# Splitting W2's products around the row scores, and one transpose for both tiles' row maxima

## What is computed

```python
x = x + _L0_xattn_ref(_layernorm(x), ctx, ...)   # 16 heads, 64 keys; then relu(out @ W1 + b1) @ W2 + b2
x = x + _L0_ffn_ref(_layernorm(x), ...)          # top 2 of 8 LoRA experts around one 256->1024->256 FFN
x = x + _L1_xattn_ref(_layernorm(x), ctx, ctx, ...)
x = x + _L1_ffn_ref(x, weight, disha)
```

```python
q = (x @ Wq + bq).reshape(B, N, NUM_HEADS, HEAD_DIM)
scores = jnp.einsum('bnhd,bmhd->bhnm', q, k) * scale
attn = jax.nn.softmax(scores, axis=-1)
out = jnp.einsum('bhnm,bmhd->bnhd', attn, v).reshape(B, N, IMAGE_DIM)
h = jax.nn.relu(out @ W1 + b1)
return h @ W2 + b2
```

## Time and profile before

| | |
|---|---|
| median of 3 runs | 336.73 us (336.33 to 340.38) |
| the profiled execution's own time | 335.96 us |
| its span in the trace | 333.9 us |
| TensorE busy (products) | 316.3 us, 95% |
| VectorE, ScalarE, GpSimd busy | 233.0, 172.2, 145.1 us |
| share of the last chain on TensorE | 86% |
| mean granted TensorE clock | 0.987 of full |

### The profile page before, as it was taken

How to read it: one execution, slowest core, us unless ns; L and a number is a source line. 1 busy time by engine, 2 the same in 40 slices (tenths; PEclk the granted TensorE clock), 3 DMA queues, 4 the chain that set the end, 5 groups by cost and what they waited for, 6 DMA issues and landing times.

```text
span 333.9 us, 6495 instructions
## 1 busy us (share of the span) xinstructions
PE 316.3 (95%) x2515; PEld 287.9 (86%) x2515; DVE 233.0 (70%) x643; ACT 172.2 (52%) x347; POOL 145.1 (43%) x149
## 2 busy tenths in 40 slices
PE   7799898999999999999999999999999999899992
PEld 5577897799998999899979997999889988899771
DVE  4865378565779577865876787767785769466666
ACT  4236826673475646572576267535755554534511
POOL 1914571635145632745072706271546234613341
PEclk9899999999999999999999999999999999999996
DMA  7879530003100130003100320032001200000000
GB/s 249 217 184 356 136 96 1 2 0 82 46 2 3 41 87 31 2 18 100 46 0 2 94 65 0 2 76 84 2 0 41 55 34 1 2 0 33 0 33 31
DMA packets 14366, 18.85 MB, mean 56 GB/s; under 512 B 2144, under 2 KB 10720, under 8 KB 14080
## 3 DMA queue, kind: packets, MB, share of 16 engines
q1 hardware_dynamic: 12464, 15.12, 16.6%
q10 hardware_dynamic: 1872, 3.31, 2.9%
HBM read 9.51 MB, written 2.62 MB: 36 GB/s over the span
## 4 chain that ended last, share of the span: by engine, by line
PE 86%; DVE 6%; ACT 4%; DMA 1%; issue 1%; POOL 0%; DVEq 0%; POOLq 0%; ACTq 0%
PE psI L289 13%; PE psP L298 13%; PE psI L298 12%; PE psI L443 12%; PE psS L298 6%; PE psT L289 4%; PE psP L380 3%; PE psS L343 3%; PE psI L605 2%; PE psS L366 2%; PE psT L313 2%; PE psP L381 2%; PE psT L510 2%; ACT qu_h L783 2%; PE psP L597 1%; DVE kb L1372 1%
## 5 line engine op out<-in xcount | busy, mean ns | idle before, releaser
L1401 POOL TENSOR_TENSOR rs<-ve,mhalf 128x2 f32<-128x2 f32 x30 | 21.9, 731 | 102.1 <-DVE ve L1027 102.1
L1420 POOL TENSOR_TENSOR hid_l<-r,hid_h 128x512 fp32r<-128x512 f32 x32 | 40.8, 1290 | 15.3 <-ACT hid_h L829 15.3
L1106 DVE SCALAR_TENSOR_TENSOR r<-psI,nbi,r 128x256 f32<-128x256 f32 x60 | 25.8, 479 | 25.2 <-PE psI L443 25.1
L443 PE MATMUL psI<-at_h,lb_h 128*128 128x256 f32 x120 | 36.5, 304 | 2.0 <-DVE at_l L1098 1.5
L1414 POOL TENSOR_TENSOR hs_l<-hs,hs_h 128x512 fp32r<-128x512 f32 x16 | 20.7, 1294 | 38.5 <-ACT hs_h L809 38.5
L443 PE MATMUL psI<-at_l,lb_h 128*128 128x256 f32 x120 | 33.8, 282 | 0.0
L443 PE MATMUL psI<-at_h,lb_l 128*128 128x256 f32 x120 | 33.8, 281 | 0.0
L1047 DVE RECIPROCAL rec<-psP 128x256 f32<-128x256 f32 x16 | 28.1, 1754 | 7.5 <-PE psP L381 7.5
L824 ACT ACTIVATE r<-psI,first 128x256 f32<-128x256 f32 x60 | 24.2, 469 | 13.6 <-PE psI L443 13.4
L443 PEld LDWEIGHTS psI<-at_h,lb_h 128*128 128x128 f32 x120 | 22.6, 188 | 8.6 <-issue 5.0
L773 ACT ACTIVATE xn<-xmid,nmr,rs 128x256 f32<-128x256 f32 x16 | 8.8, 595 | 40.9 <-POOL nmr L1405 40.9
(11 more groups left out here) (257 smaller groups left out, 866.8 us busy)
## 6 DMA issues: line engine op xcount, KB each, us to landing
stack<-qu_h SPq DMA_DIRECT2D x60, 64.0 KB, 2.0
xin<-in_x SPq DMA_DIRECT2D x8, 256.0 KB, 2.7
stack<-qu_l SPq DMA_DIRECT2D x32, 64.0 KB, 2.0
out<-x ACTq DMA_DIRECT2D x7, 256.0 KB, 2.0
raw_wi<-in_wi SPq DMA_DIRECT2D x1, 1024.0 KB, 7.6
raw_wo<-in_wo SPq DMA_DIRECT2D x1, 1024.0 KB, 13.7
kv<-in_kv SPq DMA_DIRECT2D x2, 384.0 KB, 10.6
raw_w<-in_w ACTq DMA_DIRECT2D x1, 512.0 KB, 7.2
```

The source lines that it names most:

```text
L443: last = mm(bank[:, k * T:(k + 1) * T], (WH, WL)[x]["lb"][:, 0, f * P:(f + 1) * P], AT[y][:, which, :], start=False, stop=q == 2, skip_gro ...
L1106: last = V.scalar_tensor_tensor(out=R1[:, f, :], in0=bank[:, k * T:(k + 1) * T], scalar=nbi[:, f:f + 1], in1=R1[:, f, :], op0=MAX, op1=ADD)
L1401: G_.tensor_tensor(rs[:, :], ve[:, :], mhalf[:, :], ALU.pow).then_inc(S(f"ln{j}_rs"), 1)
L1420: G_.tensor_tensor(HL[:, two, :], R1[:, two, :], as32(HH[:, two, :]), ALU.subtract).then_inc(S("hidl"), 1)
```

## The change

`a_out` is cut in two. Its first half (chunks 0 and 1 of the hidden layer, passes high x high and high x low of W2, both tiles, 8 products) stands ahead of `a_row_scores(h, 0)` and waits only for the first half of `hs_h`. The second half (8 products on chunks 2 and 3, then the 8 with `hs_l` over all chunks) stands behind them. The maxima of the two tiles, before 128x16 each, now lie in one 128x64 tile at columns 0 to 15 and 32 to 47, the rest zero; one transpose turns it, tile 1 lands on rows 32 to 47 of the bank, and ScalarE copies it with two instructions of 16x1024 in place of one of 16x2048. VectorE clears the tile once at the start, ahead of `zeros`.

```diff
+MXW = 2 * HEADS
...
-    mx = sb("mx", [P, NT * HEADS])
-    MX = r3(mx, NT)
+    mx = sb("mx", [P, NT * MXW])
+    MX = r3(mx, NT)[:, :, 0:HEADS]
...
-                for t in range(NT):
-                    last = nc.tensor.transpose(P_(1)[0:HEADS, t * P:(t + 1) * P], MX[:, t, :], ident)
-                last.then_inc(S("mxT_ps"), 1)
+                if b == 0:
+                    pe.wait_ge(S("mx_zero"), 1)
+                nc.tensor.transpose(P_(1)[0:NT * MXW, 0:P], mx[:, :], ident).then_inc(S("mxT_ps"), 1)
...
-                    pe.wait_ge(S("mstack"), b + 1)
+                    pe.wait_ge(S("mstack"), (b + 1) * NT)
...
-            def a_out(b):
-                if b == 0:
+            def a_out(b, half):
+                if b == 0 and half == 0:
                     pe.wait_ge(S("lo_wp"), 1)
                 parts = [(P_(1)[:, t * D:(t + 1) * D], x_of(HS, t * P, P), w("w2", 0, D)) for t in range(NT)]
-                pe.wait_ge(S("hsh"), (b + 1) * NDH)
-                passes(parts, range(NF1), ((0, 0), (0, 1)), True, False)
+                pe.wait_ge(S("hsh"), b * NDH + half + 1)
+                passes(parts, range(2 * half, 2 * half + 2), ((0, 0), (0, 1)), half == 0, False)
+                if half == 0:
+                    return
                 pe.wait_ge(S("hsl"), (b + 1) * NDH)
                 passes(parts, range(NF1), ((1, 0),), False, True).then_inc(S("x1_ps"), 1)
...
+                if A_:
+                    a_out(a, 0)
                 if H_:
                     a_row_scores(h, 0)
                 if A_:
-                    a_out(a)
+                    a_out(a, 1)
...
-                A(QS[3 * PW:SROWS, :, :], P_(1)[0:HEADS, 0:T].unsqueeze(1).broadcast_to([HEADS, PAIRS, T]),
-                  ACT.Identity).then_inc(S("mstack"), 1)
+                for t in range(NT):
+                    A(QS[3 * PW:SROWS, :, t * P:(t + 1) * P],
+                      P_(1)[t * MXW:t * MXW + HEADS, 0:P].unsqueeze(1).broadcast_to([HEADS, PAIRS, P]),
+                      ACT.Identity).then_inc(S("mstack"), 1)
...
             V.memset(avg[:, :], 1.0 / D).then_inc(S("avg"), 1)
+            V.memset(mx[:, :], 0.0).then_inc(S("mx_zero"), 1)
             V.memset(zeros[:, :], 0.0).then_inc(S("zeros"), 1)
```

## The result

| | before | changed |
|---|---|---|
| median of 20 runs each | 336.59 us | 334.40 us |
| the profiled execution's own time | 335.96 us | 334.57 us |
| its span | 333.9 us | 332.4 us |
| TensorE busy | 316.3 us | 316.3 us |
| mean granted TensorE clock | 0.987 | 0.994 |

The ratio of the times is 0.9923, with a 95% interval of 0.9902 to 0.9944: 2.2 us by the medians, and a small gain that is certain. TensorE does as much as before (2507 products instead of 2515; the difference is the eight transposes), so nearly all of it is waiting. From there to the turn of x2 in the body a = 7 it takes 273.74 us instead of 275.77: 2.03 us less.

The account below looks back on a forecast made before the run. TensorE, busy for 95% of the span, was taken to bound the kernel. 5 x (0.19 + 0.05) + 0.58 + 0.20 + 0.10 = 2.08 us, from 336.73, gave 334.6 us, range 332.8 to 336.6.

Parts of the forecast that it names:

- What bounds the place, and the new wait: Bodies a = 2 to 6: 0.54 us won at the row scores, 0.35 lost waiting for GpSimd's hid_l, 0.19 kept.
- GpSimd doesn't bind: Rival: GpSimd's split hs_l and hid_l are ready sooner, all waits go, 5.3 us won, 331.4 us; chance 0.10.
- The body a = 0, 0.58 us: First body: W2's low pass loads at 40.02 instead of 40.60, after waiting for hs_l; 0.58 us won.
- The body a = 7, 0.20 us: Last body, without row scores: the FFN's low pass loads at 292.81 instead of 293.01; 0.20 us won.
- The turn of x2, 0.05 us: One transpose saves 0.10 us of TensorE, but the turn waits for VectorE's x2: 0.05 us stay in each of five bodies.
- The opening, 0.1 us: Before the first real scores: the queue of fillers sets their start, so one transpose fewer gives 0.1 us once.
- Copies and clearing at nothing: ScalarE's two copies take 2.04 us, 0.17 more, with cover left; VectorE's clearing delays only fillers: 0 us.
- The sum without the opening: Five bodies at 0.19 + 0.05 us each, plus 0.58 for a = 0 and 0.20 for a = 7.
- The rule against the change: fourth_residual on VectorE and GpSimd's hid_l could hinder each other; starting order decides, they miss by 0.06 us, the sum stands.
- slower: Rival: fourth_residual, moved forward, holds back GpSimd's last hid_l by 0.44 us; 337.3 us; chance 0.06.
- All eaten: Rival: release latency and x2 take the bodies' gain, only the pipeline's ends win, 336.0 us; chance 0.14.
- It doesn't do what it says: Rival: W2's first half would have to wait for the whole hs_h; called out, with no chance given.

Follow-up runs that it names:

- two edits: Changed kernel with GpSimd's scale(4, c) moved behind hid_l, or with the FFN's first low pass moved behind the second row scores: body 34.74 and 34.73 us.
- the pair with one GpSimd step more: Changed kernel and kernel before, each with one unused GpSimd pow added behind scale(4, c): bodies 35.68 and 35.74 us, ratios to before 1.007 and 1.014.
- the second trace of before: The kernel before, run and traced again without any edit: body 35.35 us, execution 340.91 us, ratio 0.994 against itself.
- all four edits: Changed kernel with clearing later, scale(4, c) behind hid_l, low pass behind second row scores, turn of x2 later: body 34.72 us, ratio to before 0.994.

## Why the prediction was right

The forecast was 334.6 us, the result 334.4. The mechanism is as foretold, with the new wait at its place and of its size. That the time is met to 0.2 us has luck in it: the forecast started from the median of three launches, 336.73, and in the sets of launches of the experiments both kernels took some 4 us longer (340.48 and 338.45 us on one chip, again 2.03 apart). Point by point, by its own steps:

- **What bounds the place, and the new wait.** The prediction had the low pass of the FFN load 5.56 us behind the last LoRA product instead of 5.75 (188.06 and 188.25 against 182.50). Measured: 187.38 - 181.82 = 5.56. So 0.19 us were kept and the rest went into the wait, of 0.33 us between loads where 0.3 to 0.4 was foretold. That GpSimd causes it is shown from both sides: relieving it gives 0.32 to 0.36, loading it by 0.65 costs 0.60. A gain of 5 us, *GpSimd doesn't bind*, is out; two edits bring its mechanism about, and then a body gains 0.6 over before, as that rival's 0.64 has it.
- **W2's low pass and `hs_l`, 0 to 0.05 us.** The load stands 0.035 us further than the usual 0.12 from the one ahead of it.
- **The body a = 0, 0.58 us.** From the row scores to the low pass's load: 40.60 - 38.13 = 2.47 before, 40.43 - 38.54 = 1.89 now. 0.58.
- **The body a = 7, 0.20 us.** From the `hid_l` load of a = 6 to that of a = 7 it took 34.16 us before (258.85 to 293.01), and 33.94 now (257.57 to 291.51). 0.22.
- **The turn of x2, 0.05 us.** From the second tile's low pass to the turn: 192.00 to 194.53 before, 191.13 to 193.59 now, 2.53 and 2.46. It waits for VectorE by 0.05, as foretold. A body is 0.20 and 0.24 us shorter in the two profiles of the changed kernel, against 0.24 in the sum. That this term reaches the body is shown by the pair with one GpSimd step more, and not by the transpose alone, which gave nothing that can be seen.
- **The opening, 0.1 us.** Not won there. In the kernel before the fillers did set the start: the last one stands at 22.97, the first real scores at 23.00. In the changed kernel the scores start 0.35 us behind the landing of the last part of `qu_l` (23.16 and 22.82), at 23.52 and 23.17. In the kernel before it landed at 22.52, so without the fillers the scores could have started at 22.87, 0.13 us earlier at most. The prediction looked for the transpose's full 0.10 us in the wrong place: it is won in the body a = 0, where its sum has nothing for it (41.12 us before and 41.01 and 41.03 now, as above).
- **Copies and clearing at nothing.** The copies take 2.05 us (2.04 worked out) under 2.4 us of cover. The clearing costs nothing that the traces show.
- **The sum without the opening** was 1.98 us. From the first real scores to the turn of x2 in a = 7 the two profiles of the changed kernel are 2.03 and 2.24 us shorter. The match of 2.03 is partly chance. Some 0.2 us of it lie ahead of the `hid_l` of a = 1 and are in no term of that sum: the transpose's 0.10, and 0.11 between the first real scores and the row scores of a = 0 (15.13 us before, 15.02 in both profiles of the changed kernel), whose cause stays open. In the first profile the five bodies give 1.00 us where 1.20 was in the sum, which makes up for it; in the second they give 1.20.
- **The rule against the change.** The rule (the Trainium skill, SBUF — State Buffer, "Who interferes with whom") says that the order of the starts decides which of the two waits, and that the later one waits until the first is done. `hid_l` takes 1.30 us each with `fourth_residual` 0.08 us behind its end (1.29 before). The two don't overlap in any of these kernels, so no run shows what the rule would do to `hid_l`. The rival *slower* never began. But the traces do show what VectorE does to `rs`, and that it is a block and no slowing. In the opening `rs` meets `wq_l` on VectorE, a difference of two operands in SBUF. First the changed kernel, then the kernel before:

```profile
6.10 0.69 DVE L1335 TENSOR_TENSOR wq_l<-raw_wq,wq_h 128x512 fp32r<-128x512 f32 x1
6.11 1.25 POOL L1409 TENSOR_TENSOR rs<-ve,mhalf 128x2 f32<-128x2 f32 x1 [5.66 <-DVE ve L1034]
```

```profile
6.16 0.71 POOL L1401 TENSOR_TENSOR rs<-ve,mhalf 128x2 f32<-128x2 f32 x1 [5.72 <-DVE ve L1027]
6.22 0.69 DVE L1328 TENSOR_TENSOR wq_l<-raw_wq,wq_h 128x512 fp32r<-128x512 f32 x1 [0.21 <-ACT wq_h L857]
```

With VectorE first, by 0.00 to 0.10 us in four of the fourteen traces, `rs` ends 0.56 us behind the end of `wq_l`, whenever that is (1.16 to 1.25 us in all). With `rs` first, by 0.05 us or more in the other ten, it takes its 0.70 us. So far the traces agree with the rule; but `wq_l`, begun behind `rs`, takes the same 0.69 us as ahead of it, where by the rule it should have waited. Under `fourth_residual` it is the same: `rs`, at 187.58, ends 0.55 us behind the end of the instruction that had begun ahead of it, which makes the 0.86 us, and the second one, begun behind it, costs it nothing.

*All eaten* (336.0 us) would need the first wait's gain to vanish in the bodies, and they are 0.20 and 0.24 us shorter in its two profiles. *It doesn't do what it says* is out by the starts alone.

## What to carry to other kernels

A wait that is removed pays only as far as the next engine's finish: write down, for the first instructions behind it that read another engine's work, when that work ends, and add the releases (0.05 us here). The gain is the smallest of these slacks, and it put the new place of the low pass right to 0.01 us. Then look at what stands between the late engine's start and its result: here one step of 0.7 us that nobody was waiting for, whose move behind the two that TensorE needs was worth as much again as the change itself (0.3 us in a body), and nothing without it.

## What the runs showed of the hardware

- The pace of products in dense code is not fixed to better than 0.05 us in 35: the same code, from the loads of `oa_h` to the first of `hid_l`, took 11.19 us in one execution and 11.25 in another.
- A load that a semaphore releases starts 0.05 us behind the end of the releasing instruction, for GpSimd (187.33 to 187.38) as for VectorE (193.54 to 193.59).
- The opening up to the first real scores takes 23.0 to 23.5 us in three of the fourteen traces and 25.9 to 26.7 in eleven, the kernel before among both. The kept traces show what goes with it. GpSimd's `ks<-first` takes 5.37 us and holds back one of two VectorE instructions that read two operands in SBUF, `kd_h` or `kb`, whichever begins behind it. Which one it meets decides. VectorE and GpSimd in the short execution of the kernel before, then in the long one:

```profile
7.35 0.75 DVE L1332 TENSOR_TENSOR kd_h<-kt_h,first 128x256 fp32r<-128x256 f32 x2
9.40 5.37 POOL L1502 TENSOR_SCALAR ks<-first 16x2048 fp32r<-16x2048 f32 x1 [0.17 <-POOL xr L1437]
10.03 4.08 DVE L1372 TENSOR_TENSOR kb<-kt_h,first 128x1024 fp32r<-128x1024 f32 x1
```

```profile
8.70 4.22 DVE L1332 TENSOR_TENSOR kd_h<-kt_h,first 128x256 fp32r<-128x256 f32 x2
9.01 5.37 POOL L1502 TENSOR_SCALAR ks<-first 16x2048 fp32r<-16x2048 f32 x1 [0.17 <-POOL xr L1437]
12.85 0.68 DVE L1031 TENSOR_TENSOR xta_l<-psT,xta_h 128x512 fp32r<-128x512 f32 x1
```

In the three short ones both parts of `kd_h` begin ahead of `ks`; `xta_l`, which the first queries need and which has one operand in PSUM, passes beside it (9.43 us, 0.69 long, in the kernel before), and only `kb` is held. In the eleven others the second `kd_h` begins 0.03 us behind `ks` and takes 3.88 us instead of 0.42, and `xta_l` waits behind it until 12.6 us or later. What is held goes on 3.50 us behind the start of `ks` in all fourteen (its end less the 0.42 or 1.21 us that it takes alone). The short ones are those in which the GpSimd step ahead of `ks` waited for the landing of `kept`, by 0.2 to 0.7 us (at most 0.1 in the others): a load that lands later goes with an opening that is 3 us shorter. No run moves `ks`, so that this is the whole cause, and what a move would win, is not shown.
- In some executions the granted clock stood at 0.5, its level of 1.2 GHz, for 3.4 us behind the opening (27.3 to 30.7 us with one transpose alone and in the second trace of before, 28.1 to 31.5 with the clearing later), and once for 6.8 us (26.9 to 33.7, all four edits). From the first real scores to the turn of x2 in a = 7 the kernel with the clearing later took 275.00 us, the changed kernel, with the same instructions there and no such stretch, 273.74 and 273.53; the loss lies ahead of the row scores of a = 0, 16.61 us behind the first real scores instead of 15.02. What makes the clock fall there stays open. This stretch and the longer opening are as large as the effect that was measured, or larger: a comparison of two profiled times alone would have told nothing.
